# Pairs of probability tiles added on GpSimd and one ones product for the pair, Gelu per group of heads, and K sums read out of the K-X product, in a five-block transformer kernel

## The reference, cut to what matters

```python
x = x + 0.5 * fp4_ffn(layernorm(x))
# linear attention, 16 heads of 64; Q, K = elu(..) + 1
KV = einsum('bshd,bshm->bhdm', K, v)
Z  = 1 / (einsum('bshd,bhd->bsh', Q, K.sum(axis=1)) + EPS)
o  = einsum('bshd,bhdm,bsh->bshm', Q, KV, Z)
x1 = LN(src + o @ Wo + bo);  x = x + LN(x1 + gelu(x1 @ W1 + b1) @ W2 + b2)
x = x + 0.5 * fp4_ffn(layernorm(x))
x = x + 0.5 * relu_ffn(layernorm(x))
# causal attention, 16 heads: Q = x (8 wide), V 32 wide
scores = einsum('bhqd,bhkd->bhqk', Q, K) + mask
o = einsum('bhqk,bhkd->bhqd', softmax(scores), V)
x = x + gelu(o) @ Wf + bf
x = x + 0.5 * relu_ffn(layernorm(x))
```

## Time and profile before

| | |
|---|---|
| time, median of 3 runs | 1114.08 us (1111.07 to 1117.8) |
| the profiled execution's own time | 1115.28 us |
| its span, first to last instruction | 1113.5 us |
| TensorE busy | 938.3 us (84%) |
| VectorE busy | 725.9 us (65%) |
| ScalarE busy | 507.2 us (46%) |
| GpSimd busy | 291.6 us (26%) |
| mean granted TensorE clock | 0.94 |

### The profile page before, as it was taken

One profiled execution on the slowest core, in us unless ns is written; L12 is line 12 of the kernel. 1 busy time (PEld: TensorE's weight loads), 2 busy tenths in 40 slices (PEclk: granted clock), 3 DMA queues, 4 the chain that ended last, 5 costly groups with the idle time before them and its releaser, 6 DMA issues.

```text
span 1113.5 us, 19945 instructions
## 1 busy us (share of the span) xinstructions
PE 938.3 (84%) x7341; PEld 463.4 (42%) x7341; DVE 725.9 (65%) x1672; ACT 507.2 (46%) x868; POOL 291.6 (26%) x420
## 2 busy tenths in 40 slices
PE   2678888788999877568898899899899989999986
PEld 1344444456677754344333343233322223332225
DVE  7899963456887778354864577665578757677012
ACT  1132222234444323215456455756556666666772
POOL 2567762023455567500221000211000000000000
PEclk9898999999999987867998999999999999999997
DMA  6100000000000000530000400000410000000000
GB/s 197 41 1 1 0 1 1 1 1 1 2 1 1 1 1 1 105 67 2 22 22 1 99 14 17 11 2 14 84 21 11 11 1 8 13 4 11 11 1 11
DMA packets 29919, 22.68 MB, mean 20 GB/s; under 512 B 8720, under 2 KB 27008, under 8 KB 29824
## 3 DMA queue, kind: packets, MB, share of 16 engines
q1 hardware_dynamic: 28912, 20.87, 8.4%
q10 hardware_dynamic: 912, 0.54, 0.2%
HBM read 16.80 MB, written 4.34 MB: 19 GB/s over the span
## 4 chain that ended last, share of the span: by engine, by line
PE 55%; DVE 23%; POOL 7%; issue 6%; ACT 6%; DMA 2%; SPq 1%; ACTq 0%; POOLq 0%; DVEq 0%
PE psum L1618 10%; PE psum L1633 10%; PE psum L1595 6%; DVE arena L1230 6%; PE psum L1560 5%; PE psum L1507 3%; PE psum L1518 2%; PE psum L1476 2%; PE psum L1435 2%; ACT arena L913 2%; POOL rs L653 2%; DMA arena<-arena 2%; PE psum L1647 2%; DVE arena L1098 1%; PE psum L1405 1%
## 5 line engine op out<-in xcount | busy, mean ns | idle before, releaser
L1230 DVE TENSOR_REDUCE arena<-psum 128x2 f32<-128x1024 f32 (+2 forms) x320 | 335.5, 1062 | 152.3 <-PE psum L1560 78.8
L913 ACT ACTIVATE arena<-psum 128x1024 f32<-128x1024 f32 (+3 forms) x320 | 286.3, 897 | 171.6 <-PE psum L1595 95.7
L653 POOL TENSOR_TENSOR rs<-ve,mhalf 128x1 f32<-128x1 f32 x128 | 70.7, 558 | 361.0 <-DVE ve L1028 360.6
L1618 PE MATMUL psum<-arena 128*32 128x512 f32 (+3 forms) x1280 | 153.0, 551 | 1.3 <-ACT arena L913 1.3
L1633 PE MATMUL psum<-arena,ones 128*32 128x512 f32 (+3 forms) x1280 | 152.7, 550 | 0.0
L1560 PE MATMUL psum<-arena 48*128 48x512 bf16 (+3 forms) x640 | 114.3, 357 | 36.0 <-ACT arena L913 14.7
L1595 PE MATMUL psum<-arena 50*128 50x512 bf16 (+3 forms) x640 | 116.7, 361 | 11.6 <-DMA arena<-arena 4.2
L1595 PEld LDWEIGHTS psum<-arena 50*128 50x128 bf16 x640 | 31.2, 93 | 203.6 <-issue 137.1
L756 POOL TENSOR_TENSOR arena<-arena 128x512 f32<-128x512 f32 x15 | 19.1, 1272 | 230.7 <-DMA arena<-scr_sums 230.7
L1278 PE MATMUL psum<-bias_rows,onesb 128*128 128x128 bf16 (+1 forms) x128 | 38.7, 302 | 38.3 <-DVE arena L1098 19.9
L885 ACT ACTIVATE rh<-psum,fb 128x128 f32<-128x128 f32 x128 | 36.4, 369 | 58.0 <-PE psum L1507 54.0
(11 more groups left out here) (187 smaller groups left out, 1563.1 us busy)
## 6 DMA issues: line engine op xcount, KB each, us to landing
arena<-scr_parts SPq DMA_DIRECT2D x96, 64.0 KB
arena<-scr_sums SPq DMA_DIRECT2D x60, 64.0 KB, 2.0
scr_parts<-arena SPq DMA_DIRECT2D x12, 256.0 KB, 2.8
arena<-arena SPq DMA_DIRECT2D x124, 2.0 KB, 1.7
X<-in_L_attn_src_dram SPq DMA_DIRECT2D x4, 256.0 KB, 4.7
out_dram<-X SPq DMA_DIRECT2D x16, 64.0 KB, 1.6
arena<-in_c_zsel_dram SPq DMA_DIRECT2D x1, 512.0 KB, 3.7
arena<-in_L_attn_Wk_dram SPq DMA_DIRECT2D x1, 512.0 KB, 4.2
```

What stands on the lines that cost most here:

```text
L653: v.tensor_tensor(rs[:, u, t:t + 1], ve[:, u, t:t + 1], mhalf[:, :], ALU.pow).then_inc(s_rstd[u], 1)
L913: v.activation(pr[:, u % RING, pp, :, 0:CH - off], both(("scores", n))[0][:, :, off:CH], ACT.Exp).then_inc(s_p, 1)
L1230: v.tensor_reduce(MXP[:, j, 2 * pp:2 * pp + 2, m], both(("max", g, pp, j, m))[0][:, :, 0:hi - lo], AX_X, ALU.max).then_inc(s_mxd, 1)
L1618: last = mm(bank(O_BANK)[VD * h:VD * h + VD, off:CH], V[:, kb, GH * (g % GPC) + h, :], pr[:, u % RING, h // 2, h % 2, 0:CH - off], start=( ...
```

## The change

Four things are changed. (1) In the causal stage GpSimd adds the probability tiles of cells `a` and `a+1` in place (`add_probs`), for 78 pairs of the 160 cells, and the ones product is made once for each pair, in iteration `a+4`, directly behind the value product of the first half; the second half of a cell has no ones product any more. Only the last four cells of the last group keep their own. `RING` is 5 instead of 3. (2) Gelu is taken after each group instead of each chunk. (3) `G` gets a column of ones beside X in place of X's last column (`xo`, copied by ScalarE in `n_ones`), so that K sums come out of `G`; `KACC` and its 16 additions, the products against it and the copy and scaling of `KSB` are gone, and value weights are corrected once on GpSimd (`value_weights`, one 127x1024 subtraction). (4) `denominators` spreads its eight products over four column groups; `den_turn` is a product with `sel` that also sums the four.

```diff
-NORM_AT, GELU_AT = 4, 7
-RELU_START, RELU_TILE = 12, 4
+SUM_AT = 4
+INVERT_AT, NORM_AT, GELU_AT, WF_AT = 4, 6, 9, 10
+RELU_START, RELU_TILE = 14, 4
+HELD = 6
...
-        RING = 3
+        RING = 5
...
+        SUMS = sorted([(a + (SUM_AT if pair else 1), a, pair)
+                       for g in range(MGROUPS) for a in range(GROUP_U[g], GROUP_U[g + 1])
+                       for pair in [g + 1 < MGROUPS or a < GROUP_U[g + 1] - TPC]
+                       if not pair or (a - GROUP_U[g]) % 2 == 0])
...
+                    put(end + GELU_AT if end + GELU_AT <= len(CELLS) else len(CELLS), "gelu", g)
...
+            for a in PAIRED:
+                for pp in range(GP):
+                    put(a + 2, "add_probs", GP * PAIRED.index(a) + pp)
...
-                    if 0 < u <= len(CELLS):
-                        out.append(("values" if i == 0 else "sums", u - 1))
+                    if i == 0 and 0 < u <= len(CELLS):
+                        out.append(("values", u - 1))
...
+                    for when, a, _ in SUMS:
+                        if (i, u) == (0, when):
+                            out.append(("sums", a))
...
-            def sum_k(t):
-                pool.wait_ge(s_kb, t + 1)
...
-                v.tensor_tensor(KACC, KACC, Kb[t % 2], ALU.add).then_inc(s_kacc, 1)
+            def value_weights(t):
+
+                if t == 4:
+                    pool.wait_ge(s_ld["b"], 16 * 12)
+                    v.tensor_tensor(Wv[0:D - 1, :], Wv[0:D - 1, :], W7[0:D - 1, :], ALU.subtract).then_inc(s_wv, 1)
...
+            def add_probs(n):
+
+                a, pp = PAIRED[n // GP], n % GP
+                w = [CH - P * max(kb - TPC * (g // GPC), 0) for g, kb in CELLS[a:a + 2]]
+                into = pr[:, a % RING, pp, :, w[0] - w[1]:w[0]]
+                pool.wait_ge(s_av, a + 1)
+                pool.wait_ge(s_p, GP * (a + 1) + pp + 1)
+                v.tensor_tensor(into, into, pr[:, (a + 1) % RING, pp, :, 0:w[1]], ALU.add).then_inc(s_ps, 1)
...
+            def n_ones(t):
...
+                v.copy(xo[t % 2][:, 0:D - 1], XN1[:, t, 0:D - 1]).then_inc(s_xo, 1)
...
-            def gelu(c):
-                act.wait_ge(s_on, min(GPC * (c + 1), MGROUPS - 1))
+            def gelu(g):
+                o = GT[:, g % HELD, :]
+                if g + 1 < MGROUPS:
+                    act.wait_ge(s_on, g + 1)
+                    v.activation(o, o, ACT.Gelu).then_inc(s_og, 1)
+                    return
...
                 for j in range(PAIRS):
-                    mm(bank(3)[:, j:j + 1], KACC[:, P * j:P * j + P], ones1[:, 0:1], start=True, stop=True)
-                for n in range(2):
-                    last = mm(bank(6 + n), ones1[:, :], KACC[:, 512 * n:512 * n + 512], start=True, stop=True)
+                    last = mm(bank(3)[:, j:j + 1], Gs[:, P * j:P * j + P], ident[:, D - 1:D], start=True, stop=True)
...
                 for j in range(PAIRS):
-                    last = mm(bank(3)[0:H, 0:GRP], KS16[:, j, :], QT[g % 2][:, j, :],
-                              start=(j == 0), stop=(j == PAIRS - 1))
+                    q = j % 4
+                    last = mm(bank(3)[32 * q:32 * q + 32, 0:GRP], KS16[:, j, :], QT[g % 2][:, j, :],
+                              start=(j < 4), stop=(j >= 4), skip_group_check=True)
...
-                    last = nc.tensor.transpose(bank(3)[:, GRP + H * a:GRP + H * a + H], den[0:H, P * a:P * a + P],
-                                               ident[0:H, 0:H])
+                    last = mm(bank(3)[:, GRP + H * a:GRP + H * a + H], den[:, P * a:P * a + P], sel,
+                              start=True, stop=True)
```

More of the change, by code:

```diff
@@ L168, in build @@
         ebk = sb("ebk", [P, 1])
-        gains = sb("gains", [P, 4, D])
         st = sb("st", [P, 6, TILES, 6])
@@ L261, in build @@
         V = ce([TILES, H, VD])
-        RING = 3
+        RING = 5
         pr = ce([RING, GP, 2, CH])
-        GT = [ce([GPC, CH]), ce([GPC, CH])]
+        GT = ce([HELD, CH])
         DN = [ce([CH]), ce([CH])]
         DG = [ce([GH * CH // P]), ce([GH * CH // P])]
-        qkf = [ce([2, P]), ce([2, P])]
-        qkr = [ce([2, P]), ce([2, P])]
+        qkf = [early[:, 256 * n:256 * n + 256].rearrange("p (a b) -> p a b", a=2) for n in range(2)]
+        qkr = [early[:, 512 + 256 * n:768 + 256 * n].rearrange("p (a b) -> p a b", a=2) for n in range(2)]
         parts = ce([3, 2, CH], BF16)
@@ L277, in build @@
         scr = nc.dram_tensor("scr_parts", [3, 2, P, S], BF16).ap()
-        s_ld = {k: sem("ld_" + k) for k in ("x", "wr", "row", "table", "const", "b", "e")}
+        s_ld = {k: sem("ld_" + k) for k in ("x", "wr", "row", "table", "const", "b", "bv", "e")}
         s_ldx = [sem(f"ld_x{q}") for q in range(4)]
@@ L430, in causal @@
                 if g % GPC == GPC - 1:
-                    put(end + (3 if last else GELU_AT), "gelu", c)
+                    if last:
+                        put(end + 3, "gelu", g)
                     for j in range(TPC):
                         t = TPC * c + j
-                        put(end + (4 if last else GELU_AT + 1 + j), "wf", t)
+                        put(end + (4 if last else WF_AT + j), "wf", t)
                         first = end + (5 if last else RELU_START + RELU_TILE * j)
@@ L442, in causal @@
                 half = (len(maxes) + 1) // 2
-                others = [x for x in here if x[0] not in ("max", "row_max", "gelu")]
-                out += [x for x in here if x[0] in ("row_max", "gelu")]
+                others = [x for x in here if x[0] not in ("max", "row_max", "gelu", "add_probs")]
+                out += [x for x in here if x[0] in ("row_max", "gelu", "add_probs")]
                 cut = (len(others) + 1) // 2
@@ L478, in build @@
         PLAN += causal()
-        for kind in sorted({x[0] for x in PLAN} - {"quotients", "max", "invert_last"}):
+        for kind in sorted({x[0] for x in PLAN} - {"quotients", "max", "invert_last", "sums"}):
             counts = [x[1] for x in PLAN if x[0] == kind and len(x) == 2]
@@ L820, in mix_sums @@
             def mix_sums():
-                act.wait_ge(s_m, 1)
-                v.copy(KSB.rearrange("p a b -> p (a b)"), bank(6, 2)).then_inc(s_ma, 1)
-            def mix_kv():
                 act.wait_ge(s_g, TILES)
-                v.copy(Gs, bank(4, 2)).then_inc(s_ma, 1)
+                for n in range(2):
+                    v.copy(Gs[:, 512 * n:512 * n + 512], bank(4 + n)).then_inc(s_ma, 1)
             def mix_out():
@@ L959, in _ @@
             v.memset(ones1[:, :], 1.0).then_inc(s_set, 1)
-            v.memset(eps[:, :], ATT_EPS).then_inc(s_set, 1)
             v.memset(onesb[:, :], 1.0).then_inc(s_set, 1)
+            v.memset(eps[:, :], 0.0).then_inc(s_set, 1)
+            for n in range(2):
+                v.memset(xo[n][:, D - 1:D], 1.0).then_inc(s_set, 1)
             def quantise(x, y, m, s, nb, rounded):
@@ L1642, in wf @@
                 o, b, _ = both(("wf", n))
-                pe.wait_ge(s_og, n + 1)
+                pe.wait_ge(s_og, GPC * (c + 1) + (j if c + 1 == CHUNKS else 0))
                 b.free(pe)
@@ L1646, in wf @@
                 for k in range(GPC):
-                    last = mm(o[:, 0, 0:P], GT[c % 2][:, k, P * j:P * j + P], eWf[:, k, :], start=False,
+                    last = mm(o[:, 0, 0:P], GT[:, (GPC * c + k) % HELD, P * j:P * j + P], eWf[:, k, :], start=False,
                               stop=(k == GPC - 1), skip_group_check=True)
```

152 lines of the change are left out of this document (84 added, 68 removed).

## The result

The changed kernel takes **1193.55 us** (median, 1191.05 to 1196.35), the kernel before beside it 1114.4: 1.071 times as long, 95% interval 1.067 to 1.075, or +79 us. The forecast was 1153, range 1097 to 1180: the direction was right, the size was not. Half of the loss had not been priced. (One execution in the study, the profiled one of e1, ran at a granted clock of 0.72 instead of 0.90 and took 8% longer than the others of its kernel, 1252.6 us; its trace and its time are not used.)

What follows compares the result with a forecast made beforehand. TensorE was taken to bound the causal stage and second pass, VectorE the first pass; from 1115.3 us, -11 - 4 - 16 + 41 + 5 + 24 - 0.3 = +39 gave 1154, forecast 1153 us, range 1097 to 1180.

Steps and rivals of the forecast that it cites:

- parts 3 and 4: First pass without L695 -11 us, time between the passes -4, faster denominators in the second pass -16.
- Gelu by group: Causal stage: more table-load switches make M wait 2.4 us each; +24 us, +30 if the clock falls behind each.
- additions on GpSimd: Causal stage: GpSimd hides them; half of about 35 VectorE instructions wait 1.2 us, mostly in idle time; +5 us.
- The exponential that loses its cover: Causal stage: without U in the second half M waits for the exponential, 6.82 us a pair for 6.12; +41 us.
- some 80 us: Sign in the causal stage: M's wait for the exponential leads TensorE's waits, some 80 us or more, in pieces of 0.8.
- The clock rival: Causal stage: 0.84 us of idle time in every cell lowers the granted clock to 0.91; 1175 us, chance 11%.
- a chain of TensorE alone: Second pass: denominators in four column groups save 2.0 us in each of 8 groups; -16 us (-8 to -19).
- a full gain: Rival, causal stage: exponentials don't hold TensorE, a pair takes 5.2 us; 1069 us, chance 19%.
- a bound on GpSimd: Rival, causal stage: additions of over 3.4 us each make U wait; at 4 us +60 more, over 1200; chance 3%.

Runs made afterwards that it cites:

- e1: The changed kernel with the ones product of two cells moved from the first half-cell to the second: 1160.19 us, ratio 1.041.
- e4: The changed kernel with the causal stage's plan of before, except the last chunk's Gelus; five probability slots and parts 3 and 4 stay: 1083.0 us, ratio 0.977.
- e15: e7 with the steps at the places of before and the ones product two cells behind the pair's first instead of four: 1081.98 us, ratio 0.975.
- e7: e3 without the 156 GpSimd additions and their waits; denominators leave out every second cell: 1100.54 us, ratio 0.989.
- e14: e7 with the ones product of a pair in the first half-cell: 1134.43 us, ratio 1.025.
- e12: The changed kernel without its 156 GpSimd additions and their waits; denominators leave out every second cell: 1169.09 us, ratio 1.054.
- e5: The kernel before with each cell's ones product moved to the first half-cell, behind the value product, no instruction added: 1190.64 us, ratio 1.069.
- e9: e6 with VectorE's row maximum written in five reductions instead of a reduction, a copy and a subtraction: 1104.24 us, ratio 0.996.
- e10: The changed kernel with the row maximum in the same five reductions as e9: 1167.92 us, ratio 1.053.
- e6: e4 with the 156 GpSimd additions made but their results used by nothing; all 160 ones products stay: 1147.01 us, ratio 1.028.
- e13: e4 with inversion, norm, Gelu, projection and last network at the changed kernel's places, two cells later each: 1088.99 us, ratio 0.983.
- e8: e4 with the Gelu of each group by itself instead of four groups together: 1112.73 us, ratio 0.999.
- e2: The changed kernel with the Gelus of four groups done together (groups 12 to 14 together): 1165.68 us, ratio 1.046.
- e3: The changed kernel with the edits of e1 and e2 together: 1150.42 us, ratio 1.036.

## Why the prediction fell short

The runs make a ladder from the kernel before to the changed one, in us of 1114.4 times the difference of the ratios. The first step also holds the five slots and one more pair of table loads.

| step | from, to | measured | forecast |
|---|---|---|---|
| parts 3 and 4 | before, e4 | -26 | -31 |
| half the ones products, second half-cell | e4, e15 | -2 | in the +41 |
| ones product and other steps later | e15, e7 | +16 | not priced |
| ones product into the first half-cell | e7, e14 | +40 | +41 |
| Gelu by group | e14, e12 | +33 | +24 |
| additions on GpSimd | e12, changed | +19 | +5 |
| sum (before rounding) | | +79 | +39 |

Each step carries 8 to 10 us of uncertainty, since two intervals of 0.4% to 0.7% meet in it; only the second row's sign is in doubt. Two of the terms failed beyond that, the additions and the step that was left out; together they are 30 of the 40 us missed.

- **The exponential that loses its cover** was right in mechanism and size. Forecast were cells of 2.91 and 3.91 us; the rows give 2.92 and 3.78, and the wait of M leads the list with 73.7 us in 99 pieces against "some 80 us". e5 shows it alone, e14 in place, and e15 that it is not the halving that costs. But the saved 66 us of TensorE's time (152.7 to 86.0) do not come back: in e15 a cell without a ones product still takes 2.92 us for 3.07, and M's waits for exponentials are 37.8 us where e4 has 14.7. One count in the term is off without weight: the last group has six pairs and four single cells, not eight pairs.
- **The step that failed** in the forecast's own sum is the price of the additions: "half would meet an addition and wait 1.2 us on the average, 20 us on VectorE, of which most falls in its idle time. +5 us (0 to +15)". The count and the wait were near: 14 casts at +0.74, 14 subtractions at +0.91 and 12 normalisations at +0.66 us make 31 us on VectorE. What fails is "most falls in its idle time". VectorE was idle for 43% of the stage, but `row_max` is a serial chain at the end of which TensorE stands; e9 and e10 take only these instructions out of the hold and win 36 and 20 us. The share of busy time of an engine says little on a chain that passes through it. The Trainium skill (SBUF — State Buffer, Who interferes with whom) has what the rows show: a cast can contend with GpSimd, an operation with two inputs in SBUF contends with it where it reads SBUF, a reduction never does. The prediction cited it, and then did not follow the instructions that do contend to whoever waits for them. (Its row for the reduction, L1230, reads PSUM; the one of 0.22 us in e6 reads and writes SBUF.)
- **A step that was left out**: the diff moves `INVERT_AT`, `NORM_AT`, `GELU_AT`, `WF_AT`, `RELU_START` and the ones product by two to three cells. The prediction priced this at nothing without saying so. It costs 16 us (e15 to e7), of which the gather behind the loads and TensorE's wait on it are 10 to 11; e13 puts the steps without the ones product at +7, not clear of noise.
- **Gelu by group** was priced at +24 for 12 more pairs of table loads. For 11 more the runs give +25 (e8), +28 (e2) and +33 in place (e14 to e12), so the size held within the noise, though between e3 and e1 it is only 6. It held by some luck: the prediction's own figures make 5.72 - 3.13 less half a microsecond, 2.1 us each, where it takes 2.4. The rows show waits of 1.80 and 2.6 us and a lower clock behind them: between 530 and 1050 us the granted clock is 0.96 in e14 and 0.91 in e12, which differs by the Gelus alone. The forecast had this case as its upper bound, "+30 if the clock falls behind each of the 15 as well".
- **The clock rival** (0.84 us of idle time in each cell lowers the clock) had the right number, 0.89 against its 0.91, from the wrong cause: e5 has 111 of those waits and keeps 0.97. In the rows at hand the slower products stand behind waits of 1.8 us and longer, those of Gelu, of the row maximum and of the gather.
- **Parts 3 and 4**: the first pass gave 11.0 us of 11, the time between the passes 4.6 of 4. The second pass gave 24.0 - 11.0 - 4.6 = 8.4 of 16, though each `denominators` fell from 3.56 to 1.07 us, more than forecast. From the start of its first to the start of its last, before and after:

```profile
193.90:351.24 157.34, 139.05 (x876) 101.15 (x877) 107.44 (x379) 60.30 (x126) 56.60 (x91) 1.00 0.00 1
178.20:331.42 153.22, 127.81 (x890) 100.47 (x891) 107.42 (x379) 61.06 (x126) 56.56 (x91) 0.96 0.00 1
```

  The stretch is 4.1 us shorter where seven times 2.49 were saved: TensorE's idle time grew from 18.3 to 25.4 us, and its granted clock fell from 1.00 to 0.96. What was priced as "a chain of TensorE alone" waits for the others once it is faster.
- The rivals of a full gain and of a bound on GpSimd are refuted: e15 is the full gain's best case, its pair takes 5.99 us and not 5.2, and it equals e4; and no product L1680 waits for GpSimd.

What stays open is how the causes work on each other. The additions cost 52 us in e3, 24 in e2 and 19 in the changed kernel; moving the ones product costs 40 us without additions (e7 to e14) and 12 with them (e3 to e2); the Gelus cost 25 to 33 in three places and 6 in one. The order of the steps in the ladder decides how much is put to each.

## What to carry to other kernels

Before work is given to an engine that is idle on the average, list the small instructions of its neighbour that it holds (here VectorE's casts and two-input operations inside SBUF), and follow each to the one that waits for it: 28 instructions of 0.2 us cost 36 us in e6. If such work must run there, cut it into short instructions, or write the neighbour's critical steps in a form that is not held. And before an instruction is removed or moved, ask what was hidden behind it: moving the ones products by half a cell in the kernel before (e5) cost as much as the whole change, and halving their number gave nothing that could be measured. And when steps are moved, look at what their transfers now stand behind.

## What the runs showed of the hardware

- A cast or a two-input operation of VectorE inside SBUF that is issued while a GpSimd addition runs ends when that addition ends (1.94 us for 0.17, 2.27 for 0.18), and it is let in between two additions; with additions of 1.06 instead of 1.94 us the subtraction's mean fell from 1708 to 945 ns, the cast's from 1382 to 700. Reductions kept their time in all of it: 1223 ns for 1024 columns, 0.22 us for the small ones.
- In e5, 111 waits of 0.74 us on the average left the granted clock at 0.97. Behind single waits of 1.80 and 2.82 us two products took 0.61 for 0.39 us and 1.93 for 1.07.
- The gather of the denominators of group 9, four transfers of 2 KB, took 9.60 to 12.16 us behind 24 loads of 64 KB that the same engine had just issued (five kernels), and 5.89 to 7.91 us behind 12 of them (three kernels).
